# A two-layer graph network on one core: V tiles ahead of the turned weights, exponentials by pairs of heads, memory zeroed in pieces

## The chip, the cores and the metric

One of the eight cores of a Trainium2 chip runs the whole program in one launch. The metric is device microseconds of one execution. Three executions of the kernel before took 4116.4, 4117.27 and 4120.65 us; the median is 4117.27.

## The reference

The inputs are node features x (6250 x 512, float32), 100,000 edges as src and dst (sorted by dst), the weights of an attention layer with 8 heads of 64 and those of a two-layer graph convolution.

```python
h = relu(layernorm(x))
el = (h @ W_src + b_src) . attn_l      # 8 numbers per node
er = (h @ W_dst + b_dst) . attn_r
v  = h @ W_val + b_val                 # 512 per node
e  = leaky_relu(el[src] + er[dst], 0.2)
w  = exp(e - segment_max(e, dst)[dst])
x  = x + segment_sum(v[src] * w, dst) / segment_sum(w, dst)
h  = relu(layernorm(x))
twice: h = relu(dinv * segment_sum((h @ W)[src] * dinv[src], dst) + self_loop + b)
x  = x + h
```

## The kernel before

Nodes are cut into 49 tiles of 128. Edges are padded to 782 x 128; for the work on scores partition p holds the edges p * 782 to p * 782 + 781 (J = 782) with 8 heads each, so that el[:, j, h] has h innermost. The kernel is written engine by engine with semaphores; each engine carries out its list in order.

The stages around the change are these.

*Picks* (180 to 530 us in the profile). el[src] has to be found for every edge. For 560 of the 782 columns PE does it with one-hot matrices: 140 steps of 4 columns (`pick`, `pipelined`), each 48 matmuls on one of four PSUM banks (lines L1621). For each step SP loads 128 KB of `low_tab` into one of four buffers (`load_low`, L1108), four steps ahead. DVE builds one-hots (L684), multiplies and reduces (L690, L697). The other 222 columns are gathered by POOL with indirect DMAs (`collect`, L1239), paced by the count of picked steps. At step 104 (`ER_LOAD`) SP also loads `er`, 3.1 MB, from `er_tab`; DVE needs it after the picks. Behind the last `low_tab` load SP stores three small integer tables, each as 512 single elements (`need_tab`, `slot_tab`, L1112 and L1114). They are read back after the gathers.

*Scores* (530 to 640). DVE runs scans along the edges, one instruction per head (L767, L785, L799), to spread er and to find the maximum per dst. A scan has to be carried from partition to partition three times: for the maximum forwards, backwards, and for the sum of the exponentials. Each time DVE copies the tails of all partitions, PE turns them (L1657), DVE scans 128 of them in a row and PE turns the result back (L1661). L727 applies the carry. Then DVE subtracts the maximum (L803) in two halves by j, ACT takes the exponential of each half in place (L1385), SP stores each half to `w_tab` (L1121), and DVE begins the sums (L810 tails, L823 scans); `er` holds the sums, which SP stores to `sum_tab` (L1123).

*V tiles.* v = h @ W_val runs on PE tile by tile (`value`, L1566, 8 matmul records a tile) among all this: ACT drains each tile from PSUM (L1361), stores it to `v_tab` (L1365) and loads the input of the tile 4 ahead (L1317). Two SBUF rows alternate, so that draining tile t waits for the store of tile t - 2. The place of every tile in PE's list is set by hand: `V1 = 14` tiles run before the picks, `V_AT` says how many are done ahead of each of the three turns of tails, `EXP_AT` before which tile ACT does each exponential, and `W_AT` before which tile the weights are turned.

*Weights.* POOL gathers `w_tab` rows by step (L1262), after both stores of it. PE turns them (`turn_weights`, L1650, 16 groups of four 128 x 128 transposes), by turns into PSUM banks tr0 and tr1; DVE copies the even groups (L834) and ACT the odd ones (L1394) into `w_step`, which lies over `el`. `big` holds the sums of all 49 tiles and has to be zero before it is added to; it was scratch memory until then. POOL zeroes its last part early (L1258). DVE zeroes the first 10555 columns (L838), after the fourth group of weights and after `sum_tab` is stored (`er` lies in it), and another 6144 columns (L841), where `ht_ring` and two of the gathered weight rows lay, after all weights and all V tiles.

*Gather stages.* Three times POOL gathers 782 x 128 rows of 2 KB by src (`gather`, L1280): from `v_tab`, then twice from `h_tab`. For the first it waits for all V tiles' stores and for the tables; the ring has room for 12 gathers, over the memory of `rows` and `wmat`, and gather n needs the messages of gather n - 12 done. DVE multiplies rows by weights (L866, 440 steps), ACT makes one-hots (L1417, L1422), PE sums (L1673), and DVE adds to `big` (L876).

Of the kernel before, what the change touches and what calls it, by code (L numbers as in the profile page):

```python
# [9 lines left out]
ALU = mybir.AluOpType  # L10
# [4 lines left out]
P = 128  # L15
# [66 lines left out]
V_AT = (V1 + 11, V1 + 19, V1 + 29)  # L82
EXP_AT = (V1 + 25, V1 + 25)
W_AT = (V1 + 32, V1 + 32, V1 + 33, V1 + 33, V1 + 34, V1 + 34, TILES, TILES)
HT = 4
ER_LOAD = 104
# [36 lines left out]
def build(nc, x, src, dst, W_src, b_src, W_dst, b_dst, W_val, b_val, attn_l, attn_r, W1, b1, W2, b2, out):  # L123
    ctx = ExitStack()
    with ctx:
# [166 lines left out]
        ringed = part.at  # L292
        halves = [slice(half * (J // 2), (half + 1) * (J // 2)) for half in range(2)]
# [33 lines left out]
        sum_ps, half_ps = mm + tr, sm + [hist_ps, misc]  # L327
        agg_ps = sum_ps + half_ps
# [46 lines left out]
        sums_kept = sem("sums_kept")  # L375
# [53 lines left out]
        def _(dve):  # L429
# [334 lines left out]
            dve.wait_ge(er_in, 16)  # L764
# [84 lines left out]
            def aggregate_weighted(a):  # L849
                for k in range(SP + BEHIND):  # L850
# [18 lines left out]
                    if w >= 0:  # L869
                        if w % OFFS == 0:  # L870
# [228 lines left out]

# [642 lines left out]
```

## Time and profile before

| | |
|---|---|
| median of three executions | 4117.27 us |
| the profiled execution | 4112.79 us |
| its span | 4111.0 us |
| PE busy | 3449.2 us (84%) |
| DVE busy | 2248.4 us (55%) |
| ACT busy | 1772.4 us (43%) |
| POOL busy | 2673.1 us (65%) |
| mean granted TensorE clock | 0.956 |

The span is the time from the first to the last instruction in the trace. Busy shares are means over stages of different kinds. Times in views of the order of time count from the start of the span.

### The profile page before, as it was taken

What the parts mean: (1) busy time and instruction counts of PE and PEld (TensorE: products, weight loads), DVE (VectorE), ACT (ScalarE), POOL (GpSimd) and SP (SyncE); (2) the same over time, 40 slices, a digit from 0 to 9 for tenths busy, and PEclk for the clock granted to TensorE, in tenths of its full rate; (3) what the DMA queues carried; (4) which work ended last, traced back from release to release, by engine and by line L of the source; (5) the groups of instructions that cost most, each with busy time, mean ns of one, the idle gap of its engine ahead of it and who ended that gap; (6) DMA issues with size and microseconds to landing.
All of it is one profiled execution on the core that took longest, in us unless ns stands there. A gap on an engine that the chain in (4) does not pass through costs nothing.

```text
span 4111.0 us, 53570 instructions
## 1 busy us (share of the span) xinstructions
PE 3449.2 (84%) x14344; PEld 1654.0 (40%) x14344; DVE 2248.4 (55%) x3778; ACT 1772.4 (43%) x4138; POOL 2673.1 (65%) x2801
## 2 busy tenths in 40 slices
PE   5899986777888888897788888888997787888887
PEld 3499943222233333343333333333442333333332
DVE  6599886777778888883222333333552222333346
ACT  4356512444555555454333344444343333344442
POOL 3677611777777777655777777777006777777775
PEclk9999998999999999999999999999998999999999
DMA  8833335777777777665777777777117777777779
GB/s 292 245 67 62 89 98 198 210 210 210 210 210 210 210 211 210 187 205 191 210 210 210 210 210 210 210 211 210 62 67 225 210 210 210 211 210 210 211 209 352
DMA packets 318047, 802.26 MB, mean 195 GB/s; under 512 B 74753, under 2 KB 97811, under 8 KB 316801
## 3 DMA queue, kind: packets, MB, share of 16 engines
q0 software_dynamic: 201856, 631.01, 53.5%
q1 hardware_dynamic: 86421, 114.67, 8.5%
q10 hardware_dynamic: 29580, 54.49, 3.8%
q8 instruction: 66, 1.08, 0.1%
q14 instruction: 124, 1.02, 0.1%
HBM read 712.57 MB, written 88.19 MB: 195 GB/s over the span
## 4 chain that ended last, share of the span: by engine, by line
PE 32%; POOL 23%; issue 20%; DMA 13%; DVE 7%; SPq 1%; DVEq 1%; ACT 1%; POOLq 1%; ACTq 0%
POOL edge L1280 19%; PE mm L1529 8%; DMA rows_wmat<-v_tab,src_group 6%; DMA edge<-h_tab,src_group 5%; POOL rows_wmat L1280 5%; PE mm L1693 4%; PE mm L1621 4%; PE tr L1621 4%; PE sm L1693 4%; PE sm L1566 3%; DVE edge L866 2%; PE tr L1693 2%; PE tr L1524 1%; DVE big L876 1%; PE hist_ps L1693 1%
## 5 line engine op out<-in xcount | busy, mean ns | idle before, releaser
L1280 POOL DMA_INDIRECT edge<-h_tab,src_group x1564 | 1483.5, 949 | 709.8 <-issue 448.1
L1436 ACT ACTIVATE hots<-iota,drel 128x128 f32<-128x128 f32 x1760 | 538.0, 388 | 1174.8 <-PE misc L1693 587.0
L1280 POOL DMA_INDIRECT rows_wmat<-v_tab,src_group x782 | 739.3, 945 | 289.0 <-issue 218.1
L1693 PE MATMUL mm<-edge,hots 128*128 x880 | 445.6, 654 | 183.1 <-SPq L1098 173.6
L1693 PE MATMUL sm<-edge,hots 128*128 x880 | 462.1, 674 | 163.4 <-SPq L1098 159.3
L891 DVE TENSOR_TENSOR big<-big,mm 128x512 f32 x220 | 151.3, 688 | 653.3 <-PE tr L1693 634.5
L891 DVE TENSOR_TENSOR big<-big,sm 128x512 f32 x220 | 151.3, 688 | 636.6 <-PE misc L1693 623.0
L1693 PE MATMUL tr<-edge,hots 128*128 x880 | 395.6, 592 | 0.0
L1693 PEld LDWEIGHTS sm<-edge,hots 128*128 128x128 f32 x880 | 182.8, 215 | 434.7 <-issue 434.7
L1529 PE MATMUL mm<-rows_wmat 128*128 128x512 f32 x784 | 356.1, 598 | 0.0
L1693 PEld LDWEIGHTS mm<-edge,hots 128*128 128x128 f32 x880 | 175.8, 207 | 445.8 <-issue 445.6
L1673 PE MATMUL mm<-edge,hots 128*128 128x512 f32 x592 | 277.9, 608 | 63.8 <-ACT hots L1422 35.7
L1673 PE MATMUL sm<-edge,hots 128*128 128x512 f32 x584 | 277.0, 604 | 55.9 <-ACT hots L1422 27.5
L866 DVE TENSOR_TENSOR edge<-rows_wmat,tr 128x1024 f32<-128x1024 f32 x224 | 272.5, 1217 | 87.2 <-SPq L1098 87.1
L1422 ACT ACTIVATE hots<-eler_hots,ones 128x256 f32<-128x256 f32 x440 | 223.6, 508 | 205.0 <-PE sm L1673 73.8
L866 DVE TENSOR_TENSOR edge<-rows_wmat,misc 128x1024 f32<-128x1024 f32 x216 | 263.0, 1217 | 76.6 <-SPq L1098 76.5
L1417 ACT ACTIVATE eler_hots<-iota,drel 128x128 f32<-128x128 f32 x880 | 298.2, 386 | 0.0
L1239 POOL DMA_INDIRECT edge<-el_tab,src_flat x222 | 213.9, 964 | 104.0 <-issue 62.8
L1439 ACT ACTIVATE hots<-hots,ones 128x1024 f32<-128x1024 f32 x220 | 252.6, 1148 | 7.1
L1693 PEld LDWEIGHTS tr<-edge,hots 128*128 128x128 f32 x880 | 167.3, 190 | 211.9 <-issue 211.9
L1693 PE MATMUL misc<-edge,hots 128*128 x440 | 206.8, 592 | 0.0
L1693 PE MATMUL hist_ps<-edge,hots 128*128 x440 | 206.7, 592 | 0.0
(252 smaller groups left out, 4423.7 us busy)
## 6 DMA issues: line engine op xcount, KB each, us to landing
h_tab<-rows_wmat SPq DMA_DIRECT2D x98, 256.0 KB, 2.0
edge<-h_tab,src_group POOLq DMA_INDIRECT x1564, 3.7
rows_wmat<-low_tab SPq DMA_DIRECT2D x140, 128.0 KB
ht_tab<-rows_wmat SPq DMA_DIRECT2D x49, 256.0 KB
big<-ht_tab ACTq DMA_DIRECT2D x49, 256.0 KB, 2.9
v_tab<-rows_wmat ACTq DMA_DIRECT2D x49, 256.0 KB, 2.9
x_tab<-big SPq DMA_DIRECT2D x49, 256.0 KB, 2.1
rows_wmat<-v_tab,src_group POOLq DMA_INDIRECT x782, 3.7
```

Source lines behind the costliest of these rows:

```text
L866: dve.tensor_tensor(msgs[:, k % MSGS, :, :].rearrange("p c (h f) -> p c h f", f=F), got, weights.unsqueeze(3).to_broadcast([P, 2, H, F]), ...
L891: dve.tensor_tensor(big[:, ds(o, D)], big[:, ds(o, D)], agg_ps[bank][:, :], ALU.add).then_inc(a["acc_added"], 1)
L1239: pool.indirect_dma_start(el[:, at, :], None, el_tab, bass.IndirectOffsetOnAxis(ap=src_flat[:, at:at + 1], axis=0)).then_inc(el_in[n // AH ...
L1280: pool.indirect_dma_start(ring[:, 2 * u + c, :], None, tab, bass.IndirectOffsetOnAxis(ap=src_group[:, n:n + 1], axis=0)).then_inc(a["rows_ ...
L1417: act.activation(dist[:, n % 2, c, :], iota[:, :], ACT.Abs, bias=drel[:, n * 2 + c:n * 2 + c + 1], scale=-1.0).then_inc(a["dist_set"], 1)
L1422: act.activation(onehot[:, n % HOTS, :, :], dist[:, n % 2, :, :], ACT.Relu, bias=ones[:, 0:1], scale=-1.0).then_inc(a["onehot_set"], 1)
L1436: act.activation(group_hots[:, q % 2, e, :], iota[:, :], ACT.Abs, bias=drel[:, col:col + 1], scale=-1.0).then_inc(a["dist_set"], 1)
L1439: act.activation(group_hots[:, q % 2, :, :], group_hots[:, q % 2, :, :], ACT.Relu, bias=ones[:, 0:1], scale=-1.0).then_inc(a["onehot_set"], 1)
L1529: last = nc.tensor.matmul(bank, rows[:, slot, k * P:(k + 1) * P], rhs(k), start=(k == 0), stop=(k == KC - 1))
L1621: last = pe.matmul(sum_ps[bank][:, q * NA * H:(q + 1) * NA * H], src_hot[:, par, kt, q * P:(q + 1) * P], el_parts[:, part, kt, :, :], star ...
L1673: last = pe.matmul(gat_ps[w % GAT_SUMS][:, :], onehot[:, w % HOTS, n, :], msgs[:, w % MSGS, n, :], start=(n == 0), stop=(n == 1))
L1693: last = pe.matmul(agg_ps[bank][:, :], group_hots[:, q % 2, w % GROUP * 2 + n, :], edge[:, ds(slot[w % OFFS] + n * D, D)], start=(n == 0), ...
```

## The change

V tiles and weights: PE does 12, 19 and 28 tiles past `V1` ahead of the three turns of tails (11, 19 and 29 before), then all tiles that are left, and only then turns weights, into four PSUM banks instead of two. ACT drains all V tiles before it copies its first weights. Exponentials: DVE subtracts and ACT exponentiates by pairs of heads, four pieces of 782 x 2 elements, ahead of tiles 37 and 38; DVE's L810 waits for a pair before it uses it; both halves of `w_tab` are stored after all four. Zeroing: 4299 columns ahead of the weights, 8 pieces of 782 columns between the eight copies of weights, and 6144 columns by ACT, 12 pieces of 512, behind the first 12 one-hots of the first gather stage; DVE waits for these before step 18 adds up. Loads: `er` comes in four parts ahead of steps 104, 108, 112 and 116, and the three tables are stored ahead of steps 120, 124 and 128. The bound by `min` in `collect` changes nothing, since its largest value was 138 of 140.

```diff
-V_AT = (V1 + 11, V1 + 19, V1 + 29)
-EXP_AT = (V1 + 25, V1 + 25)
-W_AT = (V1 + 32, V1 + 32, V1 + 33, V1 + 33, V1 + 34, V1 + 34, TILES, TILES)
+V_AT = (V1 + 12, V1 + 19, V1 + 28)
+PAIRS = H // 2
+LATE_AT = 18
+LATE_PIECES = 12
+EXP_AT = (V1 + 23, V1 + 23, V1 + 24, V1 + 24)
-ER_LOAD = 104
+ER_LOAD = (104, 108, 112, 116)
+TABS_OUT = (120, 124, 128)
...
+        late = big[:, scanned:ringed + W_EXTRA].rearrange("p (n w) -> p n w", n=LATE_PIECES)
...
+        w_banks = [tr[0], tr[1], mm[0], mm[1]]
...
@@ vector
-            for half, at in enumerate(halves):
-                did(dve.tensor_tensor(el[:, at, :], el[:, at, :], top[:, at, :], ALU.subtract))
-                marks[f"arg{half}"] = prep[0]
-            dve.wait_ge(std_set, 4)
-            did(dve.reciprocal(dinv[:, :], small[:, 6, :]))
-
-            dve.wait_ge(w_exp, 2)
+            for pair in range(PAIRS):
+                at = slice(2 * pair, 2 * pair + 2)
+                issue(dve.tensor_tensor(el[:, :, at], el[:, :, at], top[:, :, at], ALU.subtract))
+                marks[f"arg{pair}"] = prep[0]
+            settle()
+
             for h in range(H):
+                if h % 2 == 0:
+                    dve.wait_ge(w_exp, h // 2 + 1)
                 issue(dve.scalar_tensor_tensor(er[:, :, h], pen_tail, 0.0, el[:, :, h], ALU.is_ge, ALU.mult,
                                                accum_out=tail_st[:, 0, h:h + 1]))
...
+            dve.wait_ge(std_set, 4)
+            issue(dve.reciprocal(dinv[:, :], small[:, 6, :]))
+            issue(dve.memset(big[:, J * H:scanned], 0.0))
             dve.wait_ge(w_kept, 32)
-            for b in range(CUT.blocks):
+            for i in range(0, 4 * CUT.blocks, 2):
+                b, q = divmod(i, 4)
                 n_w = min(P, SP - b * P)
-                for q in range(4):
-                    i = 4 * b + q
-                    if i % 2 == 0:
-                        dve.wait_ge(w_turned, i + 1)
-                        dve.tensor_copy(w_step[:, b * P:b * P + n_w, 4 * q:4 * q + 4],
-                                        tr[0][:, :].rearrange("p (q w) -> p w q", q=4)[:, 0:n_w, :]).then_inc(w_placed, 1)
-                if b == 0:
+                dve.wait_ge(w_turned, i + 1)
+                dve.tensor_copy(w_step[:, b * P:b * P + n_w, 4 * q:4 * q + 4],
+                                w_banks[i % 4][:, :].rearrange("p (q w) -> p w q", q=4)[:, 0:n_w, :]).then_inc(w_placed, 1)
+                if i == 0:
                     dve.wait_ge(sums_kept, 16)
-                    did(dve.memset(big[:, 0:scanned], 0.0))
+                issue(dve.memset(big[:, i // 2 * J:(i // 2 + 1) * J], 0.0))
+            settle()
             all_placed(dve)
-            dve.wait_ge(v_sum, TILES)
-            did(dve.memset(big[:, scanned:ringed + W_EXTRA], 0.0))
...
@@ sync
+            def keep_tab(n):
+                sp.wait_ge(dve_prep, marks["slots"])
+                tab, cols = ((need_tab, need_i), (slot_tab[0], slotcol_i[0]), (slot_tab[1], slotcol_i[1]))[n]
+                with nc.allow_non_contiguous_dma(reason="one step of the tables per partition"):
+                    sp.dma_start(tab.rearrange("b p -> p b"), cols[:, :]).then_inc(tabs_kept, 16)
...
-                if not s.inner and s.k == ER_LOAD:
-                    all_landed(sp, er_scattered, TILES)
-                    sp.dma_start(er.rearrange("p j h -> p (j h)"),
-                                 er_tab[0:EP, :].rearrange("(p j) h -> p (j h)", j=J)).then_inc(er_in, 16)
+                if not s.inner and s.k in ER_LOAD:
+                    n = ER_LOAD.index(s.k)
+                    at = slice(n * J * H // 4, (n + 1) * J * H // 4)
+                    if n == 0:
+                        all_landed(sp, er_scattered, TILES)
+                    sp.dma_start(er.rearrange("p j h -> p (j h)")[:, at],
+                                 er_tab[0:EP, :].rearrange("(p j) h -> p (j h)", j=J)[:, at]).then_inc(er_in, 16)
+                if not s.inner and s.k in TABS_OUT:
+                    keep_tab(TABS_OUT.index(s.k))
...
@@ scalar
-            for t in range(V1, TILES + 1):
-                for n in range(2):
-                    if t == EXP_AT[n]:
-                        exponentials(n)
-                for n, at in enumerate(W_AT):
-                    if t == at:
-                        place_odd(n)
-                if t < TILES:
-                    value(Step(t, t % HT, TILES, False))
+            for t in range(V1, TILES):
+                for pair in range(PAIRS):
+                    if t == EXP_AT[pair]:
+                        exponentials(pair)
+                value(Step(t, t % HT, TILES, False))
+            for n in range(2 * CUT.blocks):
+                place_odd(n)
...
+                    if n < LATE_PIECES:
+                        act.activation(late[:, n, :].rearrange("p (a z) -> p a z", z=P),
+                                       zeros[:, 0:P].unsqueeze(1).to_broadcast([P, AW // P, P]), ACT.Copy).then_inc(late_zeroed, 1)
...
@@ tensor, turn_weights
-                    if i >= 2:
-                        pe.wait_ge((w_placed, w_placed_odd)[i % 2], i // 2)
+                    if i >= 4:
+                        pe.wait_ge((w_placed, w_placed_odd)[i % 2], i // 2 - 1)
...
-            for n, at in enumerate(W_AT):
-                values(at - values_done[0])
+            values(TILES - values_done[0])
+            for n in range(2 * CUT.blocks):
                 turn_weights(n)
```

## Rows read from the trace of the kernel before

**Rows 1.** The page, part 4: the chain that ended last, by line.

```profile
POOL edge L1280 19%; PE mm L1529 8%; DMA rows_wmat<-v_tab,src_group 6%; DMA edge<-h_tab,src_group 5%; POOL rows_wmat L1280 5%; PE mm L1693 4%; PE mm L1621 4%; PE tr L1621 4%; PE sm L1693 4%; PE sm L1566 3%; DVE edge L866 2%; PE tr L1693 2%; PE tr L1524 1%; DVE big L876 1%; PE hist_ps L1693 1%
```

**Rows 2.** Windows: length; PE, PEld, DVE, ACT, POOL busy us; PEclk, DMA share, GB/s.

```profile
1100.00:1200.00 100.00, 80.30 (x176) 29.46 (x174) 77.24 (x87) 48.49 (x134) 75.64 (x80) 1.00 0.73 210
```

**Rows 3.** Order of time, POOL: start, us, line, out<-in, count, idle before and releaser.

```profile
706.16 0.95 POOL L1280 DMA_INDIRECT rows_wmat<-v_tab,src_group  x1 [51.12 <-DMA v_tab<-rows_wmat]
...
1682.43 0.95 POOL L1280 DMA_INDIRECT rows_wmat<-v_tab,src_group  x1 [0.30 <-issue]
```

**Rows 4.** The chain of waits in order of time, picks: start, us, what.

```profile
412.69 4.42 PE tr L1621 x96
...
425.26 10.93 DMA rows_wmat<-low_tab
...
438.00 6.20 PE mm L1621 x96
...
510.60 2.49 PE mm L1621 x54
...
524.70 5.64 PE tr L1621 x96
```

**Rows 5.** Order of time, SP's queue: three stores of tables, first and last.

```profile
507.55 0.43 SPq L1112 DMA_DIRECT2D need_tab<-need_i  x1
...
508.57 0.51 SPq L1114 DMA_DIRECT2D slot_tab_gcn<-slotcol_i_gcn  x1
```

**Rows 6.** Windows around the end of the picks.

```profile
510.00:515.00 5.00, 3.09 (x67) 2.93 (x64) 2.51 (x8) 1.33 (x2) 2.82 (x3) 1.00 0.85 3
515.00:520.00 5.00, 2.33 (x24) 2.06 (x24) 0.00 (x0) 0.00 (x0) 0.00 (x0) 0.69 0.18 1
520.00:525.00 5.00, 2.48 (x27) 2.07 (x26) 2.25 (x7) 1.53 (x3) 0.94 (x1) 0.50 0.00 0
525.00:530.00 5.00, 5.00 (x90) 5.00 (x88) 2.94 (x9) 0.52 (x1) 2.96 (x3) 0.79 0.10 3
```

**Rows 7.** Order of time, DVE, from the second turn to the first message.

```profile
610.91 0.41 DVE L713 COPY big<-misc 8x256 f32<-8x256 f32 x1 [3.54 <-PE misc L1657]
...
625.01 6.87 DVE L803 TENSOR_TENSOR edge<-edge 128x3128 f32<-128x3128 f32 x2
...
640.91 1.59 DVE L810 SCALAR_TENSOR_TENSOR big<-big,edge 128x782 f32<-128x782 f32 x1 [8.54 <-ACT edge L1385]
...
655.23 14.02 DVE L823 TENSOR_TENSOR_SCAN big<-big,carry,edge 128x782 f32<-128x782 f32 x8
...
680.56 8.85 DVE L838 MEMSET big<- 128x10555 f32 x1 [9.09 <-issue]
...
706.58 5.18 DVE L841 MEMSET big<- 128x6144 f32 x1 [1.91 <-issue]
713.75 2.35 DVE L866 TENSOR_TENSOR edge<-rows_wmat,tr 128x1024 f32<-128x1024 f32 x2 [1.99 <-SPq L1098]
```

**Rows 8.** Order of time, PE: three V tiles behind the third turn, 8 records each.

```profile
654.85 13.23 PE L1566 MATMUL sm<-rows_wmat,big 128*128 128x512 f32 x24
```

**Rows 9.** Groups, 500 to 720 us, by form: busy us, mean ns, idle before.

```profile
L727 DVE SCALAR_TENSOR_TENSOR edge<-big,carry,edge 128x782 f32<-128x782 f32 x16 | 25.0, 1650 | 0.1
L1385 ACT ACTIVATE edge<-edge 128x3128 f32<-128x3128 f32 x2 | 5.5, 2801 | 0.0
L777 DVE SCALAR_TENSOR_TENSOR edge<-edge 128x4480 f32<-128x4480 f32 x1 | 4.8, 4824 | 0.0
L834 DVE COPY edge<-tr 128x512 f32<-128x512 f32 x6 | 4.2, 692 | 8.1 <-PE tr L1650 8.0
```

**Rows 10.** Order of time, ACT: table load, a drain that waits for its store, last drain.

```profile
634.00 1.28 ACT L1385 ACT_TABLE_LOAD   x1 [0.41 <-ACT rows_wmat L1361]
...
648.63 0.60 ACT L1361 ACTIVATE rows_wmat<-sm 128x512 f32<-128x512 f32 x1 [6.27 <-DMA v_tab<-rows_wmat]
...
702.65 0.60 ACT L1361 ACTIVATE rows_wmat<-sm 128x512 f32<-128x512 f32 x1 [2.84 <-PE sm L1566]
```

More of the change, by code:

```diff
@@ L292, in build @@
         ringed = part.at
+        late = big[:, scanned:ringed + W_EXTRA].rearrange("p (n w) -> p n w", n=LATE_PIECES)
+        assert scanned // AW > LATE_AT
         halves = [slice(half * (J // 2), (half + 1) * (J // 2)) for half in range(2)]
@@ L763, in _ @@
                 to_turn(i)
-            dve.wait_ge(er_in, 16)
+            dve.wait_ge(er_in, 16 * len(ER_LOAD))
             dve.wait_ge(er_first_in, 16)
@@ L869, in aggregate_weighted @@
                     if w >= 0:
+                        if w == LATE_AT:
+                            dve.wait_ge(late_zeroed, LATE_PIECES)
                         if w % OFFS == 0:
@@ L1103, in load_low @@
                     sp.wait_ge(far_dist, s.k - 3)
-                if not s.inner and s.k == ER_LOAD:
-                    all_landed(sp, er_scattered, TILES)
-                    sp.dma_start(er.rearrange("p j h -> p (j h)"),
-                                 er_tab[0:EP, :].rearrange("(p j) h -> p (j h)", j=J)).then_inc(er_in, 16)
+                if not s.inner and s.k in ER_LOAD:
[7 more added lines that the diff above has]
+                    keep_tab(TABS_OUT.index(s.k))
                 sp.dma_start(low_all[:, s.j, :], low_tab[ds(s.k * Q, Q), :].rearrange("q n -> (q n)").rearrange(
                     "(a n) -> a n", a=1).broadcast_to([P, Q * P])).then_inc(low_in[s.j], 16)
-            pipelined(sp, PCOLS // Q, 4, 0, load_low, tail=PCOLS // Q - ER_LOAD)
-            with nc.allow_non_contiguous_dma(reason="one step of the tables per partition"):
-                sp.dma_start(need_tab.rearrange("b p -> p b"), need_i[:, :]).then_inc(tabs_kept, 16)
-                for n in range(2):
-                    sp.dma_start(slot_tab[n].rearrange("b p -> p b"), slotcol_i[n][:, :]).then_inc(tabs_kept, 16)
+            pipelined(sp, PCOLS // Q, 4, 0, load_low, tail=PCOLS // Q - ER_LOAD[0])
             all_landed(sp, el_in, GCOLS)
@@ L1119, in _ @@
                 at = slice(at.start * H, at.stop * H)
-                sp.wait_ge(w_exp, half + 1)
+                if half == 0:
+                    sp.wait_ge(w_exp, PAIRS)
                 sp.dma_start(by_part[:, at], edge[:, at]).then_inc(w_kept, 16)
@@ L1380, in _, with exponentials @@
             pipelined(act, PCOLS // Q, 4, 0, far)
-            def exponentials(half):
-                at = halves[half]
-                act.wait_ge(dve_prep, marks[f"arg{half}"])
-                act.activation(el[:, at, :], el[:, at, :], ACT.Exp).then_inc(w_exp, 1)
+            def exponentials(pair):
+                at = slice(2 * pair, 2 * pair + 2)
+                act.wait_ge(dve_prep, marks[f"arg{pair}"])
+                act.activation(el[:, :, at], el[:, :, at], ACT.Exp).then_inc(w_exp, 1)
             def place_odd(n):
@@ L1394, in place_odd @@
                 act.activation(w_step[:, b * P:b * P + n_w, 4 * q:4 * q + 4],
-                               tr[1][:, :].rearrange("p (q w) -> p w q", q=4)[:, 0:n_w, :], ACT.Copy).then_inc(w_placed_odd, 1)
-            for t in range(V1, TILES + 1):
-                for n in range(2):
-                    if t == EXP_AT[n]:
-                        exponentials(n)
-                for n, at in enumerate(W_AT):
-                    if t == at:
-                        place_odd(n)
-                if t < TILES:
-                    value(Step(t, t % HT, TILES, False))
+                               w_banks[q][:, :].rearrange("p (q w) -> p w q", q=4)[:, 0:n_w, :], ACT.Copy).then_inc(w_placed_odd, 1)
+            for t in range(V1, TILES):
[5 more added lines that the diff above has]
+                place_odd(n)
             def weights_out(n, b):
@@ L1645, in turn_weights @@
                     i = 4 * b + q
-                    if i >= 2:
-                        pe.wait_ge((w_placed, w_placed_odd)[i % 2], i // 2)
+                    if i >= 4:
+                        pe.wait_ge((w_placed, w_placed_odd)[i % 2], i // 2 - 1)
                     for k in range(4):
                         c, h = divmod(4 * q + k, H)
-                        last = pe.transpose(tr[i % 2][:, k * P:(k + 1) * P], halves[:, c, h, :], ident[:, :])
+                        last = pe.transpose(w_banks[i % 4][:, k * P:(k + 1) * P], halves[:, c, h, :], ident[:, :])
                     last.then_inc(w_turned, 1)
```

4 lines of the change are left out of this document (2 added, 2 removed).

## The prediction

> **What bounds the kernel now.** I read the chain of waits first, then the busy time of a few stretches, then the order of time between two stages. Over the run the chain lies most on POOL's gathers, line 1280 [rows 1]. In the first gather stage POOL is 75.6 us of 100 busy, DVE 77 and PE 80, and none of them is full [rows 2]: so which sets the pace has to be seen in the order of time. POOL issues its first v_tab gather at 706.16 and its last at 1682.43, with 780 between: (1682.43 - 706.16) / 781 = 1.250 us each, which is one gather's 0.95 plus the 0.30 issue gap [rows 3]. It never waits for a free slot. So this stage ends 977.5 us after it starts, whatever DVE and PE do, and what follows hangs on its end. The change touches only what lies before; its worth is the shift of the 706.16. I call that moment G.
>
> What sets G is POOL's wait of 51.12 us for the last stored V tile [rows 3]. That tile is late for reasons that I follow back: PE's place in the queue of V tiles, DVE's waits between 607 and 690, and the end of the picks at 530.34. I count two shifts: A, of the end of the picks, and B, of everything from there to G. All that follows 530 hangs on DVE and PE alone (the scans of el and er run back to back), so A goes through whole.
>
> **A: the er load in four parts and the tables in between.** PE sets the pace of the picks: 96 matmuls, two steps, in 4.42 us, bank pair after bank pair. Two gaps break it [rows 4]. First: with five pairs after 412.69 the next would begin at 412.69 + 5 x 4.425 = 434.8; it begins at 438.00, and takes 6.20 instead of 4.42. Loss 3.2 + 1.8 = 5.0 us. The chain shows the cause: a small low_tab load issued at 425.26, right behind the 3.1 MB er load, lands 10.93 us later. That cost PE 3.2, so 7.7 us of a load's way are covered by the four steps that it is issued ahead. A quarter of the er load takes a quarter of the transfer, 10.93 / 4 = 2.7 us; even with two or three for the small load itself it stays under 7.7. Parts are 4 steps = 8.85 us apart, so they don't add up. I count the first gap as gone: -5.0; bounds -5.0 (gone) and 0 (the first part alone hurts as much).
>
> Second: 54 of 96 matmuls run from 510.60, then PE stands in the middle of a step, and the two pairs end at 524.70 + 5.64 = 530.34 where 510.60 + 2 x 4.425 = 519.45 was due: 10.9 us [rows 4]. No semaphore lies in the middle of a step. At the same time DVE, ACT and POOL do nothing (all 0.00 from 515 to 520), the DMA engines are 85% busy at 3 GB/s just before, and from 507.55 to 508.57 SP has issued three stores of 512 elements of 4 bytes [rows 5, 6]. I read this as the three table stores in a row, which choke what all engines fetch. Now they go out at steps 120, 124 and 128, 8.85 us apart, each ahead of a low_tab load in SP's queue. PE ran 510.60 + 2.49 - 507.55 = 5.5 us from the first issue before it stood, and one store is a third of the traffic. From issue to the engines' return, 507.6 to 522.2, is 14.6 us, so one store has 4.9; with two or three for the low_tab load behind it that is just the 7.7 that are covered. I take 0.5 us for each store, 1.5 in all, and -10.9 for the gap; bounds: 0 for each, and 6.6 for each (a fixed 14.6 less the cover, rounded), 20 in all.
> The Trainium skill (DMA: Bandwidth & Descriptors, "Specifications") says that transfers under 512 B are done as read-modify-write; the 3 GB/s at 85% busy agrees, and by it 4-byte stores stay as dear wherever they are put.
> A = -5.0 - 10.9 + 1.5 = -14.4 us.
>
> **B: from the picks to the first gather,** in the clock of the trace before (A apart).
> 1. At 607.3 DVE asks PE to turn the tail; PE has 8 V tiles in its queue first and answers 3.54 us later [rows 7]. A tile is 3.44 us (a drain of 0.60 behind 2.84 of waiting for PE [rows 10]). Now 12 tiles stand before the first turn and 7 between it and the second, where 11 and 8 stood. PE was idle 4.5 us ahead of the first, so the additional tile is covered there; before the second it ends 3.4 us earlier. DVE's wait falls from 3.54 to the 0.75 or so of a turn: -2.8. L727 then ends at 622.2 instead of 625.0, and the second turn is done at 609.2.
> 2. The subtraction of the maxima (L803) ran as two contiguous pieces in 6.87 us, 1.09 ns an element [rows 7]. By pairs of heads it is four pieces of 1564 elements, two contiguous, then a jump of 32 bytes. The trace has no such form. L777 contiguous: 4824 ns / 4480 = 1.08 ns; L727 with a jump at every element: 1650 / 782 = 2.1 ns [rows 9]. A jump at every second element lies between; I take the middle, 1.55 ns, 2.4 us a piece, 9.7 in all (bounds 6.8 and 13.1).
> The Trainium skill (SBUF — State Buffer, "Door 1: The DMA port swizzle") says that accesses run at full rate from two hits in a 16-byte line on. The single-element 2.1 ns agrees with it; by it pairs would run at 1.08, and the sum below would be about 3 us better, more with item 5's clock.
> 3. The exponentials. ACT reached them only in its turn, at 634.00, after V tile 38; then 1.28 of table load and two of 2.80, until 640.8, while DVE stood 8.54 us [rows 7, 10]. Now the first two come before tile 37 (drained two tiles, 6.9 us, sooner), the others one tile on. Tile 36 is drained at 609.2 + 4 x 3.44 + 0.6 = 623.6, the first argument is ready at 624.6, and exponentials at 2.80 / 2 = 1.4 us follow the subtraction; the fourth ends 1.4 behind its end, 633.3. DVE starts L810 at the end of the subtraction, 622.2 + 9.7 = 631.9, instead of 640.91, and doesn't wait again, since its eight take 12.1 us. -9.0, which takes in item 1. Strided ACT could cost up to twice (2.8 a piece): the fourth then ends near 638, still ahead of its use at 641; but PE's tiles would lose some 4 us.
> 4. Tail, carry, scan L823: 655.23 becomes 646.2, and its end 669.28 becomes 660.3 [rows 7]. sum_tab's store goes out then; it landed 11.3 us after its issue (the end of L823 to DVE's memset, which waited for it, at 680.56), so at 671.6.
> 5. The V tiles. Behind the third turn stand 49 - 42 = 7 tiles (V1 + 28 = 42 are done, the last at 609.2 + 9 x 3.44 = 640.2). PE is idle for 4 us before it, as before, and after that 3 tiles took 13.23 us instead of 10.3 [rows 8]; behind the stall of the picks too PE ran at a granted 0.50, the lower level of 1.2 GHz [rows 6]. 646.2 + 7 x 3.44 + 2.9 = 673.2. ACT drains (0.6), the store lands 2.1 later and POOL starts after 0.75 (702.65 to 706.16, 3.5 in all [rows 3, 10]): G = 676.7. Before, the last tiles stood behind weight turns, which stood behind DVE's copy, which stood behind the wait for sum_tab and an 8.85 us memset [rows 7]. The V stores have to wait for w_tab's and sum_tab's traffic (a drain waited 6.27 us at 648.63 [rows 10]); two buffers hide it mostly, and I leave it at 0, with an upper bound of 5.
> B = 676.7 - 706.2 = -29.5 us (bounds -35: pairs at the contiguous rate, no half clock; and -21: 3.4 more for the pairs, 5 for the stores).
> 6. What is late next: the weights. POOL goes on for 12 gathers, 15 us, before it needs DVE's first message, 691.7. DVE: after the tiles at 673.8, eight times a copy of 0.69 [rows 9] and a memset of 782 columns at 8854 / 10555 ns = 0.66, with four PSUM banks so that PE is ahead: about 10.6 us, 684.4. The memset of 4299 columns and the reciprocal (3.6 + 0.5) lie between 660.3 and 673, in its wait. First message 2.0 later, as from 711.76 to 713.75 [rows 7], done at 687.6. 4 us to spare. The last memset, 5.18 us, goes to ACT: 12 pieces of 0.6 among the first 12 one-hots. ACT is 48.5 us of 100 busy in this stage [rows 2], 1.1 us of the 977.5 / 440 = 2.2 that a step takes; with a piece 1.7. It costs 0, and at DVE's first steps at most the 4 us that are spare.
>
> **Sum.** -14.4 - 29.5 = -43.9. The profiled execution, 4112.79 us (span 4111.0), becomes 4068.9; it stands 4.5 below the median, so against the median of 4117.27 I predict 4073.
>
> **Rivals.**
> (a) The table stores still stop the engines each time (20 us in place of 1.5). For it: the DMA engines are idle from 517 and yet the engines return only at 522 [rows 6], so part of the stall is no traffic and may come with each store. Against it: 5.5 us passed before PE stood. 4073 + 18.5 = 4092; for stalls of half that, 4083.
> (b) Jumps cost their full price on DVE and ACT, and V stores are held up: B -21 instead of -29.5, 4081.5.
> (c) The weights come too late for POOL: DVE's first message after 691.7. It decides from 4 us of delay on; if the eight rounds took twice their 10.6, it would cost 6.6: 4080. Against it: a copy took 0.69 us wherever PE's turn was ready [rows 9].
> (d) Slower: each store holds the picks for its whole 14.6 us without cover and leaves PE at half clock, as from 520 to 530 (clock 0.50 and 0.79: 2.5 + 1.0 us [rows 6]): 3 x 18.1 = 54.3 in place of 1.5, so 4073 + 52.8 = 4126. It passes the time of before from 15.3 us a store on (4073 - 1.5 + 3 x 15.3); against it is that all three together took 14.6.
>
> **How the numbers follow.** Forecast 0.62, (a) 0.17, (b) 0.10, (c) 0.05, (d) 0.03, and 0.03 for no change through something unseen. Lower end: -5.0 - 10.9 - 35 = -50.9, 4066, and 3 for the spread between executions: 4063. Upwards the range takes in (a) to (c), 4092. A change under 0.2% (8 us) is what I count as none; by the cases faster 0.94, same 0.03, slower 0.03.
>
> **What would show it.** Right: first v_tab gather near 662 (676.7 - 14.4) and the last 976 us later; picks without a gap of over 1 us near the er parts; no moment with all engines at rest behind a table store; DVE's wait before L810 under 1 us; the eight weight copies in one run behind the last V tile. Wrong, if POOL waits for messages after 12 gathers, if the picks end later than 518, or if the gathers' pace isn't 1.25 us.

## The result, and the profile after

Five executions of the changed kernel took 4090.3 to 4096.1 us, median 4093.2; five of the kernel before took 4113.0 to 4120.7, median 4117.3. The ratio is 0.9941 (95% interval 0.9928 to 0.9954), 24 us faster. 4073 was predicted, with 4063 to 4092 as the range: the direction is right, the gain is little more than half of the forecast, and the median is 1.2 us above the range.

The profiled execution took 4090.32 us (span 4088.4), 22.5 less than that of before. The chain by line has kept its shape; it answers to [rows 1]:

```profile
POOL edge L1297 19%; PE mm L1547 8%; DMA rows_wmat<-v_tab,src_group 5%; POOL rows_wmat L1297 5%; DMA edge<-h_tab,src_group 5%; PE mm L1711 4%; PE tr L1639 4%; PE mm L1639 4%; PE sm L1711 3%; PE sm L1584 2%; PE tr L1711 2%; DVE edge L873 2%; PE tr L1542 1%; DVE big L885 1%; PE hist_ps L1711 1%
```

The first and the last gather of v_tab (order of time, POOL; they answer to [rows 3]):

```profile
684.42 0.94 POOL L1297 DMA_INDIRECT rows_wmat<-v_tab,src_group  x1 [32.92 <-DVE big L846]
...
1660.57 0.95 POOL L1297 DMA_INDIRECT rows_wmat<-v_tab,src_group  x1 [0.30 <-issue]
```

(1660.57 - 684.42) / 781 = 1.250 us a gather, as before. So G, the first gather, carries the whole change: 706.16 to 684.42 is -21.7, of the -22.5 by which the two profiled executions differ. The memset named as releaser is no cause: the last V store is issued at 681.52 (below), and 2.9 us later POOL starts.

**The picks.** They begin at 202.93 before and at 205.34 now, in a part that the change doesn't touch (other kernels below began between 200.7 and 205.8, so 2.4 us is spread). They end at 530.34 and at 532.76: 327.4 us long in both. Nothing was gained. This is the chain of waits in the picks, to set beside [rows 4]:

```profile
454.99 4.43 PE mm L1639 x96
459.42 4.42 PE tr L1639 x96
463.84 4.01 PE mm L1639 x87
...
469.55 1.93 issue
...
471.97 6.00 PE tr L1639 x92
477.97 4.05 PE mm L1639 x88
482.03 1.35 issue
...
486.30 5.84 PE tr L1639 x96
492.14 4.42 PE mm L1639 x96
496.57 1.48 PE tr L1639 x32
498.04 1.87 issue
...
528.32 4.44 PE tr L1639 x96
```

The gap and the slow pair near the er load are gone. But three places have come where PE stands in the middle of a step. Two pairs from 463.84 should end at 472.69 and end at 477.97: 5.28 lost. The next two end at 492.14, 5.32 lost; the last eight at 532.76 where 492.14 + 8 x 4.425 = 527.54 was due, 5.22. Together 15.8 us, what both gaps of before cost together. The order of time on SP's queue has a table store 5 to 7 us ahead of each place:

```profile
462.58 0.38 SPq L1113 DMA_DIRECT2D need_tab<-need_i  x1
463.00 10.45 SPq L1128 DMA_DIRECT2D rows_wmat<-low_tab  x4
476.71 0.38 SPq L1113 DMA_DIRECT2D slot_tab_gat<-slotcol_i_gat  x1
...
490.87 0.38 SPq L1113 DMA_DIRECT2D slot_tab_gcn<-slotcol_i_gcn  x1
```

A window in the first of them shows all engines but the tail of one on POOL at rest, as in [rows 6]:

```profile
470.00:471.00 1.00, 0.00 (x0) 0.00 (x0) 0.00 (x0) 0.00 (x0) 0.08 (x1) 1.00 0.69 53
...
473.00:474.00 1.00, 1.00 (x15) 1.00 (x14) 1.00 (x3) 0.61 (x1) 0.14 (x1) 0.50 0.00 0
```

The second row shows a part of the loss that isn't the stop itself: PE comes back at a granted clock of 0.50. The pairs right behind the first two stops take 6.00 and 5.84 us instead of 4.42, so some 1.5 us of each 5.3 go to that.

**From the picks to G**: 151.7 us (684.42 - 532.76) instead of 175.8, so -24.1 where -29.5 was predicted. In the order of time on DVE (to set beside [rows 7]) the waits before the turns and before the exponentials are gone, and a new one of 16.96 us stands ahead of the copies of weights:

```profile
610.13 0.41 DVE L719 COPY big<-misc 8x256 f32<-8x256 f32 x1 [0.54 <-PE misc L1675]
...
624.23 6.88 DVE L810 TENSOR_TENSOR edge<-edge 128x1564 f32<-128x1564 f32 x4
631.14 1.59 DVE L817 SCALAR_TENSOR_TENSOR big<-big,edge 128x782 f32<-128x782 f32 x1
...
645.44 14.02 DVE L830 TENSOR_TENSOR_SCAN big<-big,carry,edge 128x782 f32<-128x782 f32 x8
...
681.40 0.69 DVE L842 COPY edge<-tr 128x512 f32<-128x512 f32 x1 [16.96 <-PE tr L1668]
...
693.41 2.35 DVE L873 TENSOR_TENSOR edge<-rows_wmat,tr 128x1024 f32<-128x1024 f32 x2 [1.52 <-issue]
```

The order of time on PE and on ACT shows why. These are the seven last V tiles (8 records each), and the drains that waited for a store, to set beside [rows 8, 10]:

```profile
645.30 12.23 PE L1584 MATMUL sm<-rows_wmat,big 128*128 128x512 f32 x24 [0.17 <-ACT rows_wmat L1378]
658.77 3.67 PE L1584 MATMUL sm<-rows_wmat,big 128*128 128x512 f32 x8 [1.24 <-ACT rows_wmat L1378]
666.92 5.25 PE L1584 MATMUL sm<-rows_wmat,big 128*128 128x512 f32 x8 [4.48 <-ACT rows_wmat L1378]
673.75 7.11 PE L1584 MATMUL sm<-rows_wmat,big 128*128 128x512 f32 x16 [1.58 <-ACT rows_wmat L1378]
```

```profile
644.56 0.60 ACT L1378 ACTIVATE rows_wmat<-sm 128x512 f32<-128x512 f32 x1 [8.19 <-DMA v_tab<-rows_wmat]
...
658.03 0.60 ACT L1378 ACTIVATE rows_wmat<-sm 128x512 f32<-128x512 f32 x1 [6.72 <-DMA v_tab<-rows_wmat]
...
666.18 0.60 ACT L1378 ACTIVATE rows_wmat<-sm 128x512 f32<-128x512 f32 x1 [7.56 <-DMA v_tab<-rows_wmat]
...
673.01 0.60 ACT L1378 ACTIVATE rows_wmat<-sm 128x512 f32<-128x512 f32 x1 [6.23 <-DMA v_tab<-rows_wmat]
...
681.52 0.34 ACTq L1382 DMA_DIRECT2D v_tab<-rows_wmat  x1
```

PE is fed by ACT's drains, and these by the stores two tiles back. The store issued at 651.33, for one, holds up the drain at 666.18, 14.9 us later. From 645.30 to 680.86 the seven tiles took 35.6 us, not the 27.0 of the prediction.

So there were two questions: why a table store costs PE some 5 us at each of its three places, and what makes the V tiles slow.

### The profile page after: what moved, and what is told of

Its sections match the earlier page's. It is cut to its first block, busy times and chain, and to the rows that moved or that the text cites. A ratio compares the mean times of both kernels' runs of the same rounds, so it can differ in the third digit from the quotient of the medians.

```text
span 4088.4 us, 53595 instructions
## 1 busy us (share of the span) xinstructions
PE 3440.9 (84%) x14344; PEld 1653.5 (40%) x14344; DVE 2243.1 (55%) x3787; ACT 1782.5 (44%) x4152; POOL 2673.5 (65%) x2801
## 4 chain that ended last, share of the span: by engine, by line
PE 33%; POOL 24%; issue 21%; DMA 12%; DVE 5%; SPq 1%; POOLq 1%; DVEq 1%; ACT 1%; ACTq 0%
POOL edge L1297 19%; PE mm L1547 8%; DMA rows_wmat<-v_tab,src_group 5%; POOL rows_wmat L1297 5%; DMA edge<-h_tab,src_group 5%; PE mm L1711 4%; PE tr L1639 4%; PE mm L1639 4%; PE sm L1711 3%; PE sm L1584 2%; PE tr L1711 2%; DVE edge L873 2%; PE tr L1542 1%; DVE big L885 1%; PE hist_ps L1711 1%
## 5 line engine op out<-in xcount | busy, mean ns | idle before, releaser
L1711 PE MATMUL sm<-edge,hots 128*128 x880 | 445.4, 654 | 159.9 <-SPq L1107 157.2
```

What stands on the lines that cost most here:

```text
L1711: last = pe.matmul(agg_ps[bank][:, :], group_hots[:, q % 2, w % GROUP * 2 + n, :], edge[:, ds(slot[w % OFFS] + n * D, D)], start=(n == 0), ...
```

## The experiments

Eleven more runs were made, one of them a repeat. Unless another is named, the edit is against the changed kernel. "Picks" is the time from their first matmul to their last; 311.6 us is their length without a loss (t_rows16 below, no gap at all, and the same in three more profiles with its tables), and what is above it is lost. The kernel before on the same chips took 4113 to 4116 as a median.

### t_row120: the three stores in a row again, but in the picks

```diff
                 if not s.inner and s.k in TABS_OUT:
-                    keep_tab(TABS_OUT.index(s.k))
+                    for n in range(3) if s.k == TABS_OUT[0] else ():
+                        keep_tab(n)
```

> The kernel after the change, with all three table stores in a row ahead of step 120 instead of steps 120, 124 and 128. Theory (a store of 512 single 4-byte elements starves all engines for a time that is mostly fixed per burst): one burst costs the picks about the 10.9 us of the kernel before instead of 3 x 5.2 = 15.6, so 4.7 us faster than after, 4088.5. Rival 1 (each store costs its own 5.2, wherever it is): 4093, as after. Rival 2 (the stall of before came from the end of the loop and not from the stores): under 3 us of stall here, 4080.

4087.26 us (4086.07 to 4089.99), ratio 0.9932 (0.9918 to 0.9946). The picks lose 13.7 us in one place; from the chain of waits there:

```profile
464.73 4.38 issue
...
474.44 2.56 issue
477.00 6.49 PE tr L1640 x84
```

Expected were 10.9 and 4088.5; rival 1, 4093, isn't what came. Three stores in a row lose 10.9 us in the kernel before, 12.1 in b_er4 (below) and 13.7 here; three apart lose 15.8 in the changed kernel and 21.7 in v4, which has the same picks. One profile of each, with such a spread, doesn't rank packed against spread by much, but it shows that neither helps: spreading them out leaves each stop dear, as in rival (a) of the prediction.

### t_scores: the stores behind the picks, among DVE's scans

```diff
-                if not s.inner and s.k in TABS_OUT:
-                    keep_tab(TABS_OUT.index(s.k))
...
             all_landed(sp, el_in, GCOLS)
+            for n in range(3):
+                keep_tab(n)
             load_tabs()
```

> The kernel after the change, with the three table stores after the picks and after the last el gather has landed, beside DVE's scans. Theory A (the stores slow what feeds engines with instructions, and the picks suffer since PE runs some 43 instructions a us there; DVE's scans of 1.8 us need few): the picks end 15.6 us sooner and the scores lose at most 2, so about 4078. Rival B (all engines stop wherever the stores are): the scores lose 10 to 14 us, about 4089. Rival C (the stall has nothing to do with the stores): 4093.

4084.77 us (4082.53 to 4084.82), ratio 0.9923 (0.9909 to 0.9937). That lies between theory A (4078) and rival B (4089). The picks take 311.6 us, nothing lost. But from their end to G are 162.7 us where the changed kernel has 151.7: 11 us come back. SP issued the stores from 517.55 to 518.53, and the order of time on ACT shows the drain that met them:

```profile
528.95 0.42 ACTq L1382 DMA_DIRECT2D v_tab<-rows_wmat  x1
540.85 0.60 ACT L1378 ACTIVATE rows_wmat<-sm 128x512 f32<-128x512 f32 x1 [11.92 <-DMA v_tab<-rows_wmat]
```

In the other kernels the stops began 5 to 7 us behind a store's issue, which here is 523 and after. This is the window:

```profile
523.00:530.00 7.00, 7.00 (x17) 3.10 (x17) 7.00 (x5) 1.19 (x2) 0.00 (x0) 0.99 0.21 18
```

Neither PE, with 17 matmuls of V tiles, nor DVE, with 5 instructions, stops; DVE's eight scans from 518.93 take 14.01 us (14.02 in t_rows16). PE in the picks, with a matmul each 46 ns, does stop. So theory A had the engines right and the price wrong (at most 2 us). What is late here is data: a V store of 256 KB, issued at 525.52, landed 15.2 us later, and the last of the three table stores, 2 KB, 20.0 us after its issue.

### t_rows16: the same bytes in pieces of 16

```diff
-        need_tab = dram("need_tab", [CUT.blocks, P], I32)
-        slot_tab = [dram(f"slot_tab_{name}", [CUT.blocks, P], I32) for name in ("gat", "gcn")]
+        need_tab = dram("need_tab", [P, CUT.blocks], I32)
+        slot_tab = [dram(f"slot_tab_{name}", [P, CUT.blocks], I32) for name in ("gat", "gcn")]
...
-                with nc.allow_non_contiguous_dma(reason="one step of the tables per partition"):
-                    sp.dma_start(tab.rearrange("b p -> p b"), cols[:, :]).then_inc(tabs_kept, 16)
+                sp.dma_start(tab, cols[:, :]).then_inc(tabs_kept, 16)
...
```

Each partition writes its four numbers (CUT.blocks = 4) side by side; the transposition is left to the reads behind the picks. Steps 120, 124 and 128 as in the change.

> The kernel after the change, with the tables laid out [128, 4] in DRAM, so that each store is 128 elements of 16 bytes instead of 512 of 4; they are read back with strided 4-byte reads after the picks. Same places as after (steps 120, 124, 128). If the cost goes by the number of small elements: about a quarter, 1.3 us a store, picks 11.7 us shorter, 4082. If it is a fixed cost of any store of under 512 bytes an element: 4093. If the strided reads back stop the engines as the stores do, the scores lose some us in turn.

**4076.44 us** (4074.89 to 4078.86), ratio 0.9905 (0.989 to 0.992), against 4093.2. Picks 311.6 us, with stores issued at 459.35, 468.25 and 477.14. PE in the order of time goes straight through (the ends of records overlap the next by the pipeline):

```profile
464.88 4.59 PE L1644 MATMUL tr<-big,edge 128*128 128x104 bf16 x96
469.31 4.59 PE L1644 MATMUL mm<-big,edge 128*128 128x104 bf16 x96
```

G is at 667.77, 16.7 earlier (3.2 of it spread ahead of the picks, and 2.4 are lost again behind them). So all of the 15.8 us hung on the form of the writes. A quarter of the loss, 1.3 us a store, was expected if the number of elements set it; nothing was left. The reads back of single 4-byte elements, issued from 515.47 to 520.29, don't stop DVE (8.96 us busy of the 9.00 from 515 to 524); whether they have a part in the 2.4 us no run tells.

### dose1 and dose2: which property of a store stops the engines

Built on t_rows16, with its own tables stored at steps 106, 110 and 114, so that four additional stores stand alone: "tight" is the store of before (512 numbers of 4 bytes side by side in DRAM), "apart" the same 512 numbers with 512 bytes from one to the next, "column" 128 numbers of 4 bytes side by side, "rows" 128 pieces of 16 bytes.

```diff
+DOSES = {118: 'tight', 124: 'apart', 130: 'column', 136: 'rows'}      # dose1
+DOSES = {118: 'column', 124: 'apart', 130: 'rows', 136: 'tight'}      # dose2
```

> The kernel after the change with the tables in rows of 16 bytes (which left the picks without a stall), and four stores more of the same integers into DRAM scratch, 6 steps apart: at step 118 the old form (512 elements of 4 bytes, neighbours 4 bytes apart from neighbouring partitions), at 124 the same 512 elements with 512 bytes between them, at 130 one column (128 elements of 4 bytes, adjacent), at 136 a table in rows (128 elements of 16 bytes). Theory by the number of elements: 118 and 124 stall the picks some 5 us each, 130 about 1, 136 none. Rival (writes from many DMA engines into one piece of DRAM get in each other's way): 118 stalls, 124 doesn't. Rival (any element of 4 bytes): 118, 124 and 130 alike.

> The four doses of dose1 in another order: 128 numbers of 4 bytes side by side ('column') ahead of step 118, 512 numbers of 4 bytes that lie 512 bytes apart ('apart') ahead of 124, 128 rows of 16 bytes ('rows') ahead of 130, 512 numbers of 4 bytes side by side ('tight') ahead of 136. Theory (writes of 4 bytes into one piece of DRAM get in each other's way): the loss moves with the layout; PE loses 4 to 5 us behind the last dose (its pair of banks takes over 7 us or there is a gap), 0.5 to 1 us behind the first, under 0.5 behind the second and the third. Rival (it was the place, the first dose of a row of them that is dear): 4 to 5 us behind the first dose, nothing behind the last. Picks 316.4 us long in either case; time 4080 to 4083.

dose1 took 4081.49 us, dose2 4087.52, one execution each. Losses, from the starts of PE's pairs in the order of time (two pairs are 8.85 us apart without a loss):

| store | dose1: issued, lost | dose2: issued, lost |
|---|---|---|
| tight | 458.58, 4.1 us | 500.85, 7.4 us |
| column | 489.24, 0.7 us | 454.55, 6.3 us |
| apart | 475.97, none | 474.29, none |
| rows | 503.36, none | 487.66, none |

The row of "column" in dose1 (order of time, PE), then the two places in dose2:

```profile
494.78 5.33 PE L1655 MATMUL mm<-big,edge 128*128 128x104 bf16 x96
```

```profile
460.06 0.35 PE L1655 MATMUL mm<-big,edge 128*128 128x104 bf16 x4
463.15 0.24 PE L1655 MATMUL mm<-big,edge 128*128 128x104 bf16 x1 [2.75 <-issue]
...
506.25 0.30 PE L1655 MATMUL tr<-big,edge 128*128 128x104 bf16 x3
510.02 0.91 PE L1655 MATMUL tr<-big,edge 128*128 128x104 bf16 x3 [3.47 <-issue]
511.29 6.98 PE L1655 MATMUL tr<-big,edge 128*128 128x104 bf16 x90 [0.36 <-issue]
```

The number of 4-byte elements isn't it (512 apart: nothing, 128 side by side: up to 6.3), and the first place in a row alone isn't it either, since "tight" lost 7.4 us in the last. What stops the engines are 4-byte writes side by side in one stretch of DRAM. The size of a stop isn't settled by the layout: "column" cost 0.7 once and 6.3 once, where 0.5 to 1 was expected, so dose2's picks took 325.4 us and not 316.4. Both dear first places leave it open whether the place adds to the price.

### b_er4: the kernel before with er in four parts, nothing else

```diff
-ER_LOAD = 104
+ER_LOAD = (104, 108, 112, 116)
...
+                if not s.inner and s.k in ER_LOAD:
+                    n = ER_LOAD.index(s.k)
+                    at = slice(n * J * H // 4, (n + 1) * J * H // 4)
...
```

> The kernel before the change, with the er load in four parts ahead of steps 104, 108, 112 and 116 and nothing else. Theory: the gap of 5.0 us goes, the picks take 327.4 - 5.0 = 322.4 us instead of 327.4 (first matmul to last), and the time is 4111. Rival (four parts each leave a gap of their own): 4116, as before.

4110.22 us (4105.52 to 4117.38, 12 executions) against 4113.27 of the kernel before (17): ratio 0.9991 (0.9983 to 1.0), at the edge of what can be told. The profile is clearer: picks 323.7 us instead of 327.4, the gap at er gone, and the stop by the tables 12.1 us in this execution (323.7 - 311.6) instead of 10.9. Without that difference the parts bring 3.7 + 1.2 = 4.9 us; the prediction had 5.0.

### v4: four buffers for the V tiles

Behind the picks the V tiles go round SBUF rows 0, 1, 6 and 7 instead of 0 and 1, with a semaphore each.

```diff
-                act.activation(rows[:, par, :], sm[par][:, :], ACT.Copy).then_inc(v_set, 1)
+                slot, kept = ((0, 1, 6, 7)[b], v_late[b]) if late_tile else (par, v_kept[par])
+                act.activation(rows[:, slot, :], sm[par][:, :], ACT.Copy).then_inc(v_set, 1)
...
```

> The kernel after the change, with four SBUF rows for V tiles behind the picks instead of two, so that a drain waits for the store four tiles back. Theory (V stores take 6 to 14 us while w_tab's and sum_tab's 3.2 MB are stored, and two rows make PE wait for them: the 7 tiles behind the third turn took 35.6 us instead of 24.1): they take about 26, POOL's first v_tab gather comes about 9 us sooner, 4084. Rival (another wait takes its place, such as the last stores' landing behind sum_tab's store, or the weights): less than 3 us, 4091.

4089.63 us (4084.64 to 4093.45), ratio 0.994 (0.9926 to 0.9953): no better in the median. Its profiled execution took 4084.64, although the table stores cost 21.7 us in it (picks 333.3; the three stops 7.5, 8.5 and 5.7). The seven tiles behind the third turn take 27.4 us (648.14 to 675.50) instead of 35.6, where about 26 was expected: that the wait for the store two tiles back made them slow is shown by this. From the picks to G are 144.2 us instead of 151.7: 7.5 won, of 9 expected. What is left is another late transfer, the input of a tile:

```profile
671.80 3.70 PE L1593 MATMUL sm<-rows_wmat,big 128*128 128x512 f32 x8 [2.79 <-DMA big<-ht_tab]
```

### r16_v4: both

t_rows16 with the four buffers of v4.

> Both edits that helped, on the kernel after the change: tables laid out in rows of 16 bytes, and four SBUF rows for V tiles. If they add: picks of 311.6 us, and 144 to 147 us from the end of the picks to POOL's first v_tab gather: about 4069. Rival (without the stalls something else ends last ahead of the gather, such as an ht_tab load behind sum_tab's store): 4074.

4073.21 us (4069.15 to 4081.3, six executions), ratio 0.99 (0.9885 to 0.9916). G at 664.00, 149.9 behind the picks, where t_rows16 has 154.0 and rows16_again (below) 152.7. So the edits don't add up (4069 was expected), and the rival, 4074, holds: PE now waits 5.92 us for an input behind `sum_tab`'s traffic, and part of the 7.5 comes back.

### late_sum: the store of sum_tab out of the way

t_rows16, with the 3.2 MB store of `sum_tab` behind the last V drain.

```diff
             sp.wait_ge(dve_prep, marks["sums"])
+            sp.wait_ge(v_set, TILES)
```

> The kernel after the change with the tables in rows of 16 bytes, and sum_tab's store held back until ACT has drained the last V tile. Theory (sum_tab's 3.2 MB make the V stores late and so PE's last tiles): the last four V tiles follow each other in 3.5 to 4 us, ACT waits for no V store after the third turn but the first two, and POOL's first gather comes 5 to 8 us sooner; in exchange the zeroing waits 11 us for sum_tab behind the last tile, and POOL then waits for the first messages. Rival (w_tab's rows, which POOL gathers, are what delays them): PE's tiles as late as in the kernel with the tables in rows alone.

4076.23 us, one execution. The last V tile is done at 660.1, 145.8 us behind the picks, instead of 664.05 (150.3; 149.0 in rows16_again), so `sum_tab`'s traffic costs the tiles 3 to 5 us. But the drains still wait 8.16 and 5.61 us for V stores at 641.35 and 647.56, with POOL's gathers from `w_tab` (4.2 MB from 628.8 to 648) and the tiles' own inputs beside them. So the theory holds for a part, and the rival for the rest. And the late store then meets the last V stores and DVE (order of time, POOL, then DVE):

```profile
670.40 0.95 POOL L1303 DMA_INDIRECT rows_wmat<-v_tab,src_group  x1 [34.89 <-DMA v_tab<-rows_wmat]
```

```profile
670.73 0.71 DVE L846 MEMSET big<- 128x782 f32 x1 [9.21 <-DMA sum_tab<-big]
```

G isn't earlier: 156.0 us behind the picks, where t_rows16 has 154.0. What the tiles win by the later store, the last V stores lose; a third place for it wasn't tried.

### halves and rows16_again: the exponentials by pairs undone

t_rows16 with the two contiguous halves of before, ahead of V tile 37; each half of `w_tab` is stored behind its exponential again. rows16_again is t_rows16 once more, beside it.

```diff
-EXP_AT = (V1 + 23, V1 + 23, V1 + 24, V1 + 24)
+EXP_AT = (V1 + 23, V1 + 23)
...
-                if half == 0:
-                    sp.wait_ge(w_exp, PAIRS)
+                sp.wait_ge(w_exp, half + 1)
...
```

> t_rows16 with one thing undone: the maxima are subtracted and the exponentials taken in two contiguous halves as before, the exponentials put behind V tile 23 of the stage. Theory: the pairs are worth the exponentials' time only: the second half's exponential (2.8 us) ends 2.8 behind the subtraction and the first product of DVE needs both halves: DVE waits 2.5 to 4 us ahead of it where it waits none with pairs, the sums end 2.5 to 4 us later, and the time is 4078 to 4080 against t_rows16's 4076.4. Rival (the V stores set the end, and the sums are hidden): DVE waits just as long ahead of the first product, but the first v_tab gather stays within 1 us of t_rows16's distance from the picks (154.1 us) and the time within 1 us of 4076.4. Second rival (ACT's table load and 2.8 us of exponentials at once stop its drains and with them PE): 5 us or more, 4081.

> The kernel of t_rows16 once more, as the neighbour on the same chip of the one with halves: 4074 to 4079, first v_tab gather 153 to 155 us behind the picks' end, no stall in the picks (311.6 us).

halves: **4071.5 us** (4069.47 to 4073.61), ratio 0.9896 (0.988 to 0.9913). rows16_again: 4076.52 (4070.82 to 4079.33), ratio 0.9906 (0.9889 to 0.9922). The intervals overlap, so only this is shown: the pairs bring nothing. That they cost some 4 us is likely (seven of the eight executions with pairs, on two chips, lie above the slowest of halves), but not shown. In the profile DVE waits before the products, as expected, and the drains behind it wait as ever (order of time, DVE and ACT of halves):

```profile
615.64 1.59 DVE L814 SCALAR_TENSOR_TENSOR big<-big,edge 128x782 f32<-128x782 f32 x1 [2.95 <-ACT edge L1403]
```

```profile
636.16 0.60 ACT L1379 ACTIVATE rows_wmat<-sm 128x512 f32<-128x512 f32 x1 [7.12 <-DMA v_tab<-rows_wmat]
```

Counted from the end of the picks, the sums end 2.6 us later than in rows16_again (129.9 and 127.3 us), and yet G comes 2.7 us earlier (150.0 and 152.7). So the theory, 4078 to 4080, fails, and the rival in which the sums are hidden holds in its mechanism but not in its numbers: G's distance was to stay within 1 us of t_rows16's 154, and the time within 1 us of 4076.4. A likely part of it: with halves SP stores `w_tab` from 612.11 on, with pairs at 619.03, and that traffic too meets the V stores. One profile each doesn't settle that.

## Why the prediction was wrong, and where it was right

Of the 43.9 us forecast for the profiled execution 22.5 came. The missing 21.4 are 14.4 of A (picks as long as before), 5.4 of B (24.1 instead of 29.5) and 2.4 of spread ahead of the picks, less 0.8 behind G.

1. **"PE sets the pace of the picks", gap at er -5.0**: right. No gap there in the profile after; alone it brought 4.9 (b_er4).
2. **"I take 0.5 us for each store, 1.5 in all"**: this step failed. 15.8 us in all, and the sign named for it came: the picks end later than 518, at 532.76. I divided the 14.6 us from issue to return by three, as if the stop were traffic that follows the number of elements, and set the low_tab loads' 7.7 us of cover against it. But from the first issue at 462.58 to PE's pair at 471.97 one store has 9.4 us, not 4.9, and three in a row have 14.6 in the kernel before and 17.4 in t_row120 (459.64 to 477.00); the cover is of no use, since PE doesn't lack low_tab data but stands within a step. (The upper bound has a slip: 14.6 - 7.7 is 6.9, not 6.6.) The half clock behind each stop, some 1.5 us, wasn't in the 0.5 either; only rival (d) had it. Rival (a), stalls that come each time, held 0.17 and named the mark that I had seen: DMA engines idle from 517 and the engines back only at 522 [rows 6]. Its price was 20 us and the time 4092; measured 15.8 and 4093.2. The bounds (0 and 6.6 a store) held the 5.3 of this profile, but not the 7.5 and 8.5 in v4 nor the 7.4 in dose2.
 From the Trainium skill's rule on transfers under 512 B (DMA: Bandwidth & Descriptors, "Specifications") the prediction drew that 4-byte stores stay as dear wherever they are put. Within the picks the trace agrees (5.28, 5.32 and 5.22 us). The rule doesn't tell dear from cheap, though: pieces of 16 bytes, and 4-byte pieces 512 bytes apart, are under 512 B as well and lost nothing.
3. **B1, the second turn's wait**: right, 0.54 us instead of 3.54 [rows 7].
4. **B2, the pairs' subtraction**: I took 9.7 us between 6.8 and 13.1; it took 6.88, as long as the contiguous halves (6.87 [rows 7]). The middle of two rows was the wrong choice. The Trainium skill's rule (SBUF — State Buffer, "Door 1: The DMA port swizzle") that two hits in a 16-byte line are enough agrees with the trace.
5. **B3, exponentials**: in mechanism right, no wait before L817; 1.62 us a piece, where 1.4 was forecast. With 4, the V tiles behind the third turn began 112.5 us behind the picks (645.30 - 532.76) where 115.9 was forecast. But halves shows that nothing of it reaches G.
6. **B5, "The V stores have to wait ... I leave it at 0, with an upper bound of 5"**: the second failed step. Seven tiles took 35.6 us and not 27.0: 8.6 us, and four rows bring them to 27.4 (v4). I had one such wait in the rows (6.27 us [rows 10]) and believed that two buffers hide the others. With a store's usual 2.9 us to landing (the page after, part 6) that would be so; beside the 3.2 MB stores and POOL's gathers of w_tab, with the DMA engines over 90% busy from 640 to 670, a V store took 7 to 15 us. B1 to B3 brought 3.4 more than forecast and this took 8.6: that is the 5.3 by which G, counted from the picks, is late.
7. **B6, weights late next**: they weren't. First message 9.0 us behind G (693.41 - 684.42), where 15 were allowed, although they are turned only behind the tiles. ACT's zeroing cost nothing.
8. **The gather stage's pace and what follows**: right, 1.250 us, G + 976.2 to the last.
9. **The other rivals.** (b): the half with the V stores came, 8.6 us where it had 5; jumps cost DVE nothing. (c): no, by 7. (d), slower: no. A stop costs some 5 us (8.5 at most, in v4), not 18; its half clock was real.

The median is 4093.2, within 1.2 us of rival (a)'s time. Its mechanism came, but that the number fits so well is luck: its 20 us were 4.2 too many, and B fell short by 5.4 that it didn't have. The forecast had the right list of events and the wrong price for two.

## What to carry to other kernels

When all engines rest at once, look for one cause for all; before it is moved, find out what of it is fixed per event: dividing it by the number of stores, and setting cover against the rest, gave a tenth of the true price, while another layout for 6 KB of stores took away all 15.8 us. When work is packed tighter in front of a wait for "all stores landed", price the stores at their time beside the bulk transfers that share the moment, not at their time alone; and shifting one of those transfers may only move the loss, as in late_sum. An engine's earlier finish is worth nothing until the chain to the end passes through it: with the V stores last, the faster exponentials had no worth.

## What the runs showed of the hardware

- 512 (or 128) writes of 4 bytes side by side in DRAM stop PE, ACT and mostly DVE and POOL, from 5 to 7 us behind their issue on; in the picks PE lost 4.1 to 8.5 us each time that such a store stood alone (once 0.7), and 10.9 to 13.7 for three in a row. Beside the few and long instructions of the scores PE and DVE didn't stop (t_scores). 512 such writes 512 bytes apart, or 128 of 16 bytes side by side, stop nothing. That the stop is one of instruction supply fits two things: matmuls pass one at a time at its edges, and long instructions run on through it (t_scores). But the page after (part 3: queue, kind, packets, MB, share of the engines) has two queues of instructions among the DMA queues, and neither has a packet between 424 and 549 us, where all three stops lie; in the kernel before and in dose2 too none starts within 30 us ahead of a stop or within it. So a late packet of these queues isn't what the engines wait for. What they do wait for stays open.

```profile
q8 instruction: 66, 1.08, 0.1%
q14 instruction: 124, 1.02, 0.1%
```

- V stores of 256 KB landed in a median of 2.9 us, but in 7 to 15 beside such stores or 3.2 MB ones.
- DVE works on pairs of float32 with 32 bytes from one pair to the next at the rate of contiguous data (6.88 against 6.87 us for 6256 elements). For ACT that isn't shown: four exponentials of 1564 such elements took 1.62 us each, 6.5 in all, two contiguous ones of 3128 2.80 each, 5.6 in all; how much of the 0.9 is a fixed time of each instruction no run tells.
